# A vision tower with routed experts on one core: token rows read in pieces and turned by VectorE's block transpose, not by products with the identity

## The chip, the core and the metric

One Trainium2 chip (trn2), one of its cores. The metric is the device time of one execution in microseconds, and the figure of the kernel is the median of its runs: 129.36 us before the change, of three runs from 128.86 to 130.53. Five engines take part: TensorE (PE: products), VectorE (DVE), ScalarE (ACT), GpSimd (POOL), and SyncE (SP), whose queue issues most DMAs. Each engine has its own instruction list and waits for the others by semaphores.

## The reference

Sixteen images of 96 x 96 x 3 are cut into 36 patches of 16 x 16 x 3 and projected to 256 features; a class token is put ahead, so there are 16 x 37 = 592 tokens. One attention block (16 heads of 16, causal), and one block of eight experts follow, each over the layer-normalised tokens, each added to its input. The last is what the change touches:

```python
x = layernorm(h).reshape(-1, 256)
red = x @ w_red
logits = red @ (wg / max(norm(wg), 1e-4)).T        # 8 experts
idx = argmax(softmax(logits)); scores = softmax(logits)[idx]
hid = gelu(x @ w1[idx] + b1[idx])                  # 256 -> 1024
y = hid @ w2[idx] + b2[idx]                        # 1024 -> 256
out = h + y * scores
```

Everything is float32. Each token goes to one expert only, so the kernel sorts the tokens by expert and gives each expert the rows it needs.

## The kernel before, in words

It is one program with one hand-written instruction list an engine; no scheduler moves anything. Its stages are the embedding, the first normalisation with value rows, keys and queries, a loop over eight pairs of images (attention), the second normalisation with the choice of the expert, the dispatch, and the expert stage.

**Slots.** A token's row in `hz` holds 640 floats: the residual row h (256), the normalised row z (256), and 128 more, of which the first is the token's number and the second its score (`ROW`, L58). Each expert has a region of `slot_scratch` in DRAM. At the start SyncE clears 112 rows of each region from `nil` (L340). GpSimd scatters the rows of all tokens to their slots (`spread`, L1228). When all five scatters have landed, SyncE reads 112 slots of every expert, 2560 bytes a row, to one buffer an expert (`load_rows`, L363; experts 2, 3, 0, 1, then 4 to 7). `CAP` = 112 slots are a tile; more tokens for an expert would give further tiles, which are behind a condition.

**Experts 0 and 1** do not wait for that: `dispatch` makes their turned rows by products on chip, into `xt`. For **experts 2 to 7** TensorE must turn the normalised half of the rows, slots on partitions, into features on partitions: `turn_rows` (L792 to L801) multiplies by the identity, four products of 64 columns by 112, each "x2" in the trace. VectorE copies the result from PSUM to `xt` (`rows_turned`, L1103 to L1108), which has two buffers.

**The expert stage on TensorE** is `hidden(t)` (L803 to L822: 32 products with w1, moving operand `xt` with 112 columns) and `down(t)` (L824 to L836: 16 products with w2, 256 columns). ScalarE's Gelu stands between. The order is hidden 0, 1, down 0, 1, hidden 2, and then hidden(t), down(t - 1) for t from 3 on. `turn_rows(2)` stands in the middle of `down(1)`, `turn_rows(3)` behind it, and `turn_rows(t + 1)` between `hidden(t)` and `down(t - 1)`. VectorE's `result(t)` (L1110 to L1125) adds bias, score and residual row, which it reads from the gathered rows; GpSimd scatters it to `out` (L1233).

**Weights.** w1 and w2 of an expert are 1 MB each, in a ring of four. Those of experts 0 to 3 are issued during attention; `load_expert(t)` for t from 4 on waits until `down(t - 4)` is done (`y_ps`, L334). All of it is on SyncE's queue, behind the row loads.

**The values** take a path over DRAM: `hz` to `v_scratch` (L344), and back in six loads each half, three of 32 rows by 8 images and three of 5 rows by 8 images (L350; `SPLIT`, L82). **The bias products** (L578 to L582) make a bias of the expert choice from `boutc`; VectorE copies it (L1030).

Of the kernel before, what the change touches and what calls it, by code (L numbers as in the profile page):

```python
# [20 lines left out]
P = 128  # L21
# [23 lines left out]
CAP = 112  # L45
HALVES = ((0, 64), (64, CAP))
# [11 lines left out]
ROW = 2 * D + 128  # L58
# [69 lines left out]
def vit_tower(nc, embed_in, places_in, b_proj, w_qkv, b_qk, b_v, w_out, w_out_t, b_out, b_out_c, wg, w_red_t, w1, b1, w2, b2,  # L128
              cf_d, cb_d, iota_d, out):
    ctx = ExitStack()  # L130
    with ctx:
# [75 lines left out]
        hz = sb("hz", [P, NT, ROW])  # L207
# [5 lines left out]
        hz_id = hz[:, :, :].bitcast(U32)[:, :, 2 * D]  # L213
        hz_score = hz[:, :, 2 * D + 1]
# [36 lines left out]
        xt = late(2 * KD * CAP).rearrange("p (b k n) -> p b k n", b=2, k=KD)  # L251
        yout = pos[:, 0:2, :]
        hsum = sb("hsum", [P, 2, D])

        def row_of(t):
            r = t % E
            return rows[0:CAP, r, :] if r < RING else more[0:CAP, r - RING, :]
# [5 lines left out]
        vrow = hz[:, :, 0:D]  # L263
        v3 = [w[0:GS, RING - 1, :, :].rearrange("p a b -> p (a b)").rearrange("p (b d) -> p b d", d=D)
# [16 lines left out]
        def o_bank(u):  # L281
# [13 lines left out]
            xt_ps xt_ready hidden_ps gelu_ready y_ps y_ready  # L295
# [8 lines left out]
        gathered = [sem(f"gathered{t}") for t in range(E)]  # L304

# [13 lines left out]
        def _(sp):  # L319
# [20 lines left out]
            sp.dma_start(of_expert[0:CAP, :, :], nil[0:CAP, :].unsqueeze(1).to_broadcast([CAP, E, ROW]))\  # L340
# [21 lines left out]
            def load_rows(t):  # L362
                sp.dma_start(row_of(t), of_expert[0:CAP, t, :]).then_inc(gathered[t], 16)  # L363

            sp.wait_ge(q["spread"], 16 * NT)
            for t in (*range(ONCHIP, RING), *range(ONCHIP), *range(RING, E)):
                load_rows(t)
            for t in range(RING, E):
                load_expert(t)
            sp.wait_ge(q["meta_ready"], 1)  # L370
            n = sp.value_load(meta[0:1, 2 * OVF:2 * OVF + 1], min_val=0, max_val=OVF)
            with sp.If(n > 0):
                for t in range(E):
                    sp.wait_ge(gathered[t], 16)
                for i in range(OVF):
                    sp.dma_start(of_expert[(i + 1) * CAP:(i + 2) * CAP, :, :], nil[0:CAP, :].unsqueeze(1).to_broadcast([CAP, E, ROW]))\
                      .then_inc(q["spill_cleared"], 16)
                sp.wait_ge(q["spread"], 16 * 2 * NT)
            for i in range(OVF):
                with sp.If(n > i):  # L380
                    e = sp.value_load(meta[0:1, i:i + 1], min_val=0, max_val=E - 1)
                    row = sp.value_load(meta[0:1, OVF + i:OVF + i + 1], min_val=0, max_val=(E + 1) * APART - CAP)
# [3 lines left out]
                                 w1[bass.ds(e, 1)].rearrange("o (k p) f -> p (o k) f", p=P)).then_inc(loaded_w1[r], 16)  # L386
# [7 lines left out]
                    sp.dma_start(row_of(E + i), slot_d[bass.ds(row, CAP), :]).then_inc(gathered[i], 16)  # L394
# [4 lines left out]
        def _(act):  # L399
# [109 lines left out]
            for t in range(ONCHIP):  # L509
                act.wait_ge(q["soon_ps"], KD * t + 1)  # L510
                nc.scalar.activation(xt[:, t, 0, :], ps[:, BX[t][0], 0:CAP], ACT.Copy).then_inc(q["soon0_ready"], 1)
# [28 lines left out]
        def _(pe):  # L540
# [26 lines left out]
            for j in range(NT):  # L567
# [3 lines left out]
                if j == NT - 2:  # L571
# [71 lines left out]
            turn_normalised(1)  # L643
            value_rows(0)
# [667 lines left out]
```

## Time and profile before

| | us |
|---|---|
| median of the runs | 129.36 |
| range of the three runs | 128.86 to 130.53 |
| the profiled execution, its time | 130.33 |
| its span, from the first to the last instruction | 128.4 |
| TensorE busy in it | 120.5 |
| VectorE, ScalarE, GpSimd busy | 56.7, 48.1, 42.7 |

The time holds 1.9 us that lie around the span. TensorE's granted clock is 0.999 of full speed (2.4 GHz) over the whole span. In the views an engine's name with a q (SPq) is its queue of DMA issues; "ps<-early,w1s" reads as output and inputs; early, wide, w1s, w2s and hz are memory on chip, and `early` holds the row buffers of experts 0 to 3, `gt` and `xt` in this stage, `wide` the row buffers of 4 to 7. A wait's releaser is what ended it. The mean duration of a product overlaps its neighbours, so the length of a stage is read from the chain of waits, not from the sum of means.

### The profile page before, as it was taken

The numbers are of one execution on the slowest core, as the hardware profiler recorded it, in microseconds if no ns is written. First come the engines' busy times: TensorE is split into PE (matmuls) and PEld (weight loads), VectorE is DVE, ScalarE is ACT, GpSimd is POOL, SyncE is SP. The second block draws the span as 40 slices with busy tenths as digits, with TensorE's granted clock in tenths as the row PEclk, the third lists the DMA queues.
The fourth block names the chain that finished last, engine by engine and source line by source line (L and its number), as shares of the span: only waits on it lengthen the run. The fifth ranks groups of instructions, "written<-read, shape, count | busy, mean of one in ns | idle before, by whom it ended". The sixth has DMA issues, their size and how long they took to land.

```text
span 128.4 us, 3559 instructions
## 1 busy us (share of the span) xinstructions
PE 120.5 (94%) x1460; PEld 102.0 (79%) x1460; DVE 56.7 (44%) x178; ACT 48.1 (37%) x145; POOL 42.7 (33%) x58
## 2 busy tenths in 40 slices
PE   7969999999999999999999899999999999999970
PEld 2747887877667878798799798899898999999850
DVE  1140599661996858798987300160212121220210
ACT  0300002447486666666456760036333150606000
POOL 8800014590059039272857800032020202011022
PEclk9999999999999999999999999999999999999999
DMA  4899999137919999999999947999999999200011
GB/s 114 289 334 385 390 405 394 67 125 174 171 36 205 149 269 360 390 365 379 365 402 369 362 141 212 321 298 343 381 378 384 362 388 333 68 5 25 3 29 31
DMA packets 19681, 32.75 MB, mean 255 GB/s; under 512 B 1779, under 2 KB 13686, under 8 KB 19662
## 3 DMA queue, kind: packets, MB, share of 16 engines
q1 hardware_dynamic: 18126, 30.06, 72.2%
q0 software_dynamic: 768, 2.12, 4.6%
q10 hardware_dynamic: 768, 0.31, 0.9%
q8 instruction: 13, 0.21, 0.7%
q14 instruction: 6, 0.05, 0.1%
HBM read 27.41 MB, written 5.38 MB: 255 GB/s over the span
## 4 chain that ended last, share of the span: by engine, by line
PE 68%; DMA 15%; issue 8%; POOL 3%; SPq 2%; ACT 1%; DVE 1%; POOLq 0%
PE ps L818 18%; PE ps L834 16%; PE ps L543 9%; DMA w2s<-v_scratch 6%; DMA early<-embed_in 5%; DMA v_scratch<-hz 4%; PE ps L734 4%; PE ps L602 4%; PE ps L690 3%; PE ps L703 3%; PE ps L609 3%; PE ps L799 2%; POOL vbd L1186 2%; PE ps L672 2%; POOL out L1233 1%
## 5 line engine op out<-in xcount | busy, mean ns | idle before, releaser
L834 PE MATMUL ps<-w2s,early 128*64 128x256 f32 (+1 forms) x256 | 29.2, 379 | 0.0
L525 ACT ACTIVATE early<-ps,b1s 128x112 f32<-128x112 f32 x64 | 17.4, 354 | 30.4 <-PE ps L818 30.4
L818 PE MATMUL ps<-early,w1s 128*64 128x112 f32 x512 | 26.1, 259 | 0.5 <-issue 0.5
L818 PEld LDWEIGHTS ps<-early,w1s 128*64 128x64 f32 x512 | 25.6, 137 | 1.0 <-issue 0.8
L834 PEld LDWEIGHTS ps<-w2s,early 128*64 128x64 f32 (+1 forms) x256 | 23.1, 130 | 3.4
L543 PE MATMUL ps<-early 128*128 128x256 f32 x60 | 15.0, 403 | 1.3 <-DMA early<-embed_in 1.2
L543 PEld LDWEIGHTS ps<-early 128*128 128x128 f32 x60 | 11.6, 200 | 4.1 <-DMA early<-embed_in 2.6
L1106 DVE COPY early<-ps 128x224 f32<-128x224 f32 x6 | 2.4, 392 | 24.4 <-PE ps L799 24.4
L1233 POOL DMA_INDIRECT out<-pos,early x4 | 3.8, 943 | 24.7 <-DVE pos L1124 24.4
L1233 POOL DMA_INDIRECT out<-pos,wide x4 | 3.8, 942 | 20.0 <-DVE pos L1124 20.0
L609 PE MATMUL ps<-xnt,wqkv 128*128 128x296 f32 x32 | 9.1, 422 | 0.0
L935 DVE TENSOR_REDUCE negmax<-ps 101x16 f32<-101x592 f32 x8 | 6.2, 774 | 5.8 <-PE ps L635 5.7
L410 ACT ACTIVATE xnt<-ps 128x256 f32<-128x256 f32 x5 | 1.7, 381 | 17.7 <-PE ps L589 17.7
L1158 POOL TENSOR_TENSOR rstd<-veps,cf 128x1 f32<-128x1 f32 x5 | 3.2, 632 | 15.4 <-DVE veps L883 15.4
L1124 DVE SCALAR_TENSOR_TENSOR pos<-ps,wide,hsum 112x256 f32<-112x256 f32 x4 | 1.9, 484 | 13.7 <-issue 13.7
L690 PEld LDWEIGHTS ps<-vbd,probst 111*64 111x64 f32 (+1 forms) x192 | 6.1, 125 | 1.4 <-issue 0.9
L609 PEld LDWEIGHTS ps<-xnt,wqkv 128*128 128x128 f32 x32 | 5.8, 190 | 1.8 <-issue 0.2
L690 PE MATMUL ps<-vbd,probst 111*64 111x51 f32 (+2 forms) x192 | 6.7, 215 | 0.4
L447 ACT ACTIVATE probs<-probs 101x592 f32<-101x592 f32 x8 | 5.6, 697 | 3.0 <-DVE probs L939 2.9
L1186 POOL TENSOR_TENSOR vbd<-w1s,cf 111x512 f32<-111x512 f32 x4 | 4.1, 1056 | 7.8 <-DMA w1s<-v_scratch 7.8
L672 PE MATMUL ps<-cf,probs 101*111 101x101 f32 x48 | 6.2, 266 | 0.2 <-ACT probs L447 0.2
L479 ACT ACTIVATE probst<-ps 111x303 f32<-111x303 f32 x16 | 5.9, 428 | 1.3 <-PE ps L672 1.3
(141 smaller groups left out, 172.7 us busy)
## 6 DMA issues: line engine op xcount, KB each, us to landing
w1s<-w SPq DMA_DIRECT2D x8, 1024.0 KB, 9.9
w2s<-w SPq DMA_DIRECT2D x8, 1024.0 KB, 12.7
early<-embed_in SPq DMA_DIRECT2D x5, 448.0 KB, 7.8
slot_scratch<-nil SPq DMA_DIRECT2D x1, 2240.0 KB, 14.6
early<-slot_scratch SPq DMA_DIRECT2D x4, 280.0 KB, 4.1
wide<-slot_scratch SPq DMA_DIRECT2D x4, 280.0 KB, 6.3
b2s<-b SPq DMA_DIRECT2D x4, 256.0 KB, 7.8
wqkv<-w_qkv SPq DMA_DIRECT2D x1, 768.0 KB, 11.0
```

The lines of the kernel that those rows point to most:

```text
L447: nc.scalar.activation(probs[:, u % 2, 0:ALLS], probs[:, u % 2, 0:ALLS], ACT.Exp).then_inc(q["probs_ready"], 1)
L479: nc.scalar.activation(probst[:, u % 2, half * GH * ROWS:(half + 1) * GH * ROWS], ps[0:GS, BP + half, 0:GH * ROWS], ACT.Copy).then_inc(q[" ...
L525: nc.scalar.activation(gt[:, t % 2, f, :], ps[:, 2 * (t % 2) + f // 4, (f % 4) * CAP:(f % 4 + 1) * CAP], ACT.Gelu, bias=b1t[:, f:f + 1]).t ...
L543: return nc.tensor.matmul(ps[:, j, 0:D], emb[:, k, D + j * P:D + (j + 1) * P], emb[:, k, 0:D], start=(k == 0), stop=(k == KE - 1))
L609: m = nc.tensor.matmul(ps[:, QK_BANK[a][n], 0:HALF], wqkv[:, k, col:col + P], xnt[:, k, a * HALF:(a + 1) * HALF], start=(k == 0), stop=(k ...
L672: m = nc.tensor.transpose(ps[0:GS, BP + half, g * ROWS:(g + 1) * ROWS], probs[:, u % 2, at:at + GS], ident[0:ROWS, 0:ROWS])
L690: m = nc.tensor.matmul(ps[a * ROW_B:a * ROW_B + w, o_bank(u), g * GH * VW:g * GH * VW + n], probst[:, u % 2, at:at + w], vbd[:, col:col + ...
L818: m = nc.tensor.matmul(ps[a * ROW_B:(a + 1) * ROW_B, 2 * (t % 2) + f // 4, (f % 4) * CAP:(f % 4 + 1) * CAP], w1s[:, r, k, c:c + ROW_B], xt ...
L834: m = nc.tensor.matmul(ps[n0:n1, 4 + t % 2, 0:D], gt[:, t % 2, f, n0:n1], w2s[:, r, f, :], start=(f == 0), stop=(f == FT - 1))
L935: link(V.tensor_reduce(negmax[:, u % 2, :].rearrange("p (r h) -> p r h", r=2), s3, AX.X, ALU.max, negate=True))
L1186: pool.tensor_tensor(vbd[:, 2 * u * VI:2 * (u + 1) * VI].rearrange("p (h w) -> p h w", w=VW)[:, :, 0:DH], v3[g][:, b0:b0 + 2, :].rearrange ...
L1233: pool.indirect_dma_start(out, bass.IndirectOffsetOnAxis(row_of(t).bitcast(U32)[:, 2 * D:2 * D + 1], 0), yout[0:CAP, t % 2, :], None, boun ...
```

## The change

- **Rows by pieces.** In a token's row the 128 extra floats now stand ahead, with the number at 127 and the score at 126 (`AHEAD`), so that score, number and residual row are 258 floats in a row. For experts from 2 on the normalised half comes by a load of its own, `load_blocks`: 128 slots, each cut into 4 runs of 64 floats (256 bytes), so that partition 32 b + a holds the run b of slots 4 a to 4 a + 3. `load_rows` brings the other 258 floats (1032 bytes) of 112 slots, for experts from 2 on in the order i, a of slot 4 a + i. Experts 0 and 1 read them in the plain order.
- **The turning** is one STREAM_TRANSPOSE of VectorE an expert, 128 x 256, blocks of 32 x 32, from the buffer straight to `xt`; `turn_rows` and its semaphore are gone. `xt` has 128 columns instead of 112, in four runs of 32 of which 28 are read. A feature's place is now 2 p + k, so w1 of these experts is loaded as "(p k) f", 8 KB in a row for each partition.
- **The order of the queue.** Blocks of 2 and 3 and rows of 0 to 3 come first; those of 4 and 5 behind the weights of 4, those of 6 and 7 behind the weights of 5.
- **Clearing** takes 128 slots of each expert instead of 112.
- **The bias products** move from the embedding to behind `turn_normalised(1)`. These are the four small products of the trace (two instructions, "x4").

```diff
+QB = 32
+NQ = P // QB
+CA = CAP // NQ
...
-ROW = 2 * D + 128
+AHEAD = 128
+ROW = AHEAD + 2 * D
...
-        xt = late(2 * KD * CAP).rearrange("p (b k n) -> p b k n", b=2, k=KD)
+        xt = late(2 * KD * P).rearrange("p (b k n) -> p b k n", b=2, k=KD)
...
+        def slots_of(t, k):
+            if t < ONCHIP:
+                return xt[:, t, k, 0:CAP]
+            return xt[:, t % 2, k, :].rearrange("p (i a) -> p i a", i=NQ)[:, :, 0:CA]
...
-                sp.dma_start(w1s[:, r, :, :], w1[t].rearrange("(k p) f -> p k f", p=P)).then_inc(loaded_w1[r], 16)
+                of_chunks = "(k p) f -> p k f" if t < ONCHIP else "(p k) f -> p k f"
+                sp.dma_start(w1s[:, r, :, :], w1[t].rearrange(of_chunks, p=P)).then_inc(loaded_w1[r], 16)
...
-            sp.dma_start(of_expert[0:CAP, :, :], nil[0:CAP, :].unsqueeze(1).to_broadcast([CAP, E, ROW]))\
+            sp.dma_start(of_expert[0:P, :, :], nil[:, :].unsqueeze(1).to_broadcast([P, E, ROW]))\
...
-            def load_rows(t):
-                sp.dma_start(row_of(t), of_expert[0:CAP, t, :]).then_inc(gathered[t], 16)
+            def load_blocks(t, slots):
+                sp.dma_start(blocks_of(t).rearrange("p (i n) -> p i n", i=NQ),
+                             slots[:, AHEAD + D:ROW].rearrange("s (b n) -> b s n", b=NQ)).then_inc(blocks_in[t % E], 16)
+
+            def load_rows(t, slots):
+                cols = slice(AHEAD - 2, AHEAD + D)
+                if t < ONCHIP:
+                    sp.dma_start(row_of(t)[:, cols], slots[0:CAP, cols]).then_inc(gathered[t], 16)
+                else:
+                    sp.dma_start(row_of(t)[:, cols], slots[0:CAP, cols].rearrange("(a i) n -> i a n", i=NQ))\
+                      .then_inc(gathered[t % E], 16)
 
             sp.wait_ge(q["spread"], 16 * NT)
-            for t in (*range(ONCHIP, RING), *range(ONCHIP), *range(RING, E)):
-                load_rows(t)
+            for t in range(ONCHIP, RING):
+                load_blocks(t, of_expert[0:P, t, :])
+            for t in range(RING):
+                load_rows(t, of_expert[0:P, t, :])
             for t in range(RING, E):
                 load_expert(t)
+                if t < RING + 2:
+                    for a in (2 * t - RING, 2 * t - RING + 1):
+                        load_blocks(a, of_expert[0:P, a, :])
+                        load_rows(a, of_expert[0:P, a, :])
...
-                    pe.wait_ge(q["loaded_boutc"], 16)
-                    for k in range(KD):
-                        m = nc.tensor.matmul(bo_ps, boutc[:, k:k + 1].to_broadcast([P, P]), Gc[:, k, :],
-                                             start=(k == 0), stop=(k == KD - 1))
-                    m.then_inc(q["wg_ps"], 1)
...
             turn_normalised(0)
             turn_normalised(1)
+            pe.wait_ge(q["loaded_boutc"], 16)
+            for k in range(KD):
+                m = nc.tensor.matmul(bo_ps, boutc[:, k:k + 1].to_broadcast([P, P]), Gc[:, k, :],
+                                     start=(k == 0), stop=(k == KD - 1))
+            m.then_inc(q["wg_ps"], 1)
             value_rows(0)
...
-            def turn_rows(t):
-                pe.wait_ge(gathered[t % E], 16 * (t // E + 1))
-                if t >= ONCHIP + 2:
-                    pe.wait_ge(q["xt_ready"], t - ONCHIP - 1)
-                for k in range(KD):
-                    for a in range(2):
-                        c = D + k * P + a * ROW_B
-                        m = nc.tensor.matmul(ps[a * ROW_B:(a + 1) * ROW_B, 6 + t % 2, k * CAP:(k + 1) * CAP],
-                                             row_of(t)[:, c:c + ROW_B], ident[0:CAP, 0:CAP], start=True, stop=True)
-                m.then_inc(q["xt_ps"], 1)
...
-                                w1s[:, r, k, c:c + ROW_B], xt[:, t % 2, k, :], start=(k == 0), stop=(k == KD - 1))
+                                w1s[:, r, k, c:c + ROW_B], slots_of(t, k), start=(k == 0), stop=(k == KD - 1))
...
-                    if t == 1 and f == FT // 2:
-                        turn_rows(2)
...
-            turn_rows(3)
             hidden(2)
             for t in range(3, E):
                 hidden(t)
-                if t + 1 < E:
-                    turn_rows(t + 1)
...
             def rows_turned(t):
-                dve.wait_ge(q["xt_ps"], t - ONCHIP + 1)
+                dve.wait_ge(blocks_in[t % E], 16 if t < E + ONCHIP else 32)
                 dve.wait_ge(q["hidden_ps"], 2 * (t - 1))
-                V.tensor_copy(xt[:, t % 2, :, :],
-                              ps[:, 6 + t % 2, 0:KD * CAP].rearrange("p (k n) -> p k n", k=KD))\
-                    .then_inc(q["xt_ready"], 1)
+                V.transpose(xt[:, t % 2, :, :].rearrange("p k (i a) -> p k i a", i=NQ),
+                            blocks_of(t).rearrange("p (i c k) -> p k i c", i=NQ, c=QB)).then_inc(q["xt_ready"], 1)
```

SyncE's queue from the wait for the scatter on, before (x4 and x8 are counts; `slot_scratch` is the slots in DRAM):

```order
L335 DMA w1s<-w 128x2x1024
L336 DMA w2s<-w 128x8x256
L363 DMA early<-slot_scratch 112x640 x4
L363 DMA wide<-slot_scratch 112x640 x4
L335 DMA w1s<-w 128x2x1024
L336 DMA w2s<-w 128x8x256
L335 DMA w1s<-w 128x2x1024
L336 DMA w2s<-w 128x8x256
```

and with the change (shapes are those of the side that is written):

```order
L381 DMA early<-slot_scratch 128x4x64 x2
L387 DMA early<-slot_scratch 112x258 x2
L389 DMA early<-slot_scratch 112x1x258 x2
L353 DMA w1s<-w 128x2048
L354 DMA w2s<-w 128x8x256
L381 DMA wide<-slot_scratch 128x4x64
L389 DMA wide<-slot_scratch 112x1x258
L381 DMA wide<-slot_scratch 128x4x64
L389 DMA wide<-slot_scratch 112x1x258
L353 DMA w1s<-w 128x2048
L354 DMA w2s<-w 128x8x256
```

Eight whole loads stood ahead of the weights of expert 4; now six smaller ones do, and four stand between the weights of 4 and those of 5. The same four follow behind the weights of 5.

TensorE from the embedding's last products to the first value rows, before:

```order
L543 MATMUL ps<-early 128x256 x12
L576 MATMUL ps<-wqkv,woutt 128x8 x4
L580 MATMUL ps<-wqkv,boutc 128x8 x2
L543 MATMUL ps<-early 128x256 x3
L589 MATMUL ps<-cf,hz 128x128 x4
L602 MATMUL ps<-wqkv,xnt 128x264 x2
```

and with the change:

```order
L579 MATMUL ps<-early 128x256 x12
L612 MATMUL ps<-wqkv,woutt 128x8 x4
L579 MATMUL ps<-early 128x256 x3
L620 MATMUL ps<-cf,token_rows 128x128 x4
L677 MATMUL ps<-wqkv,boutc 128x8 x2
L633 MATMUL ps<-wqkv,xnt 128x264 x2
```

The two products with `boutc` moved behind the turning of two tiles and stand ahead of the first value rows.

## Rows read from the trace of the kernel before

**Rows 1.** The page: busy time, 40 slices, issues (KB each, us to landing).

```profile
span 128.4 us, 3559 instructions
...
PE 120.5 (94%) x1460; PEld 102.0 (79%) x1460; DVE 56.7 (44%) x178; ACT 48.1 (37%) x145; POOL 42.7 (33%) x58
...
PE   7969999999999999999999899999999999999970
...
DMA  4899999137919999999999947999999999200011
...
w1s<-w SPq DMA_DIRECT2D x8, 1024.0 KB, 9.9
...
early<-slot_scratch SPq DMA_DIRECT2D x4, 280.0 KB, 4.1
```

**Rows 2.** The chain of waits, expert stage: start us, us, what.

```profile
...
81.18 0.39 PE ps L799 x8
...
83.68 6.14 PE ps L818 x128
89.82 0.39 PE ps L799 x8
90.20 3.46 PE ps L834 x32
93.66 3.07 PE ps L818 x64
...
107.47 3.07 PE ps L818 x64
```

**Rows 3.** VectorE's timeline: start us, us, engine, line, operation, tiles, count, idle before.

```profile
...
97.15 0.39 DVE L1106 COPY early<-ps 128x224 f32<-128x224 f32 x1 [2.91 <-PE ps L799]
...
100.66 0.48 DVE L1124 SCALAR_TENSOR_TENSOR pos<-ps,early,hsum 112x256 f32<-112x256 f32 x1 [2.73 <-issue]
```

**Rows 4.** SyncE's queue, timeline of its DMA issues: start us, us.

```profile
...
25.78 0.37 SPq L344 DMA_DIRECT2D v_scratch<-hz  x1
...
76.88 1.76 SPq L363 DMA_DIRECT2D early<-slot_scratch  x4
...
80.56 0.64 SPq L335 DMA_DIRECT2D w1s<-w  x1
...
83.33 2.32 SPq L335 DMA_DIRECT2D w1s<-w  x1
...
93.69 0.37 SPq L335 DMA_DIRECT2D w1s<-w  x1
```

**Rows 5.** DMA view of 76.8 to 79 us, busy tenths in 40 slices.

```profile
...
DMA  0000000000000000000995773907256979699999
```

**Rows 6.** DMA view of 94 to 98 us.

```profile
...
DMA packets 1105, 1.47 MB, mean 367 GB/s; under 512 B 27, under 2 KB 987, under 8 KB 1105
```

**Rows 7.** DMA view of 34 to 37.3 us, busy tenths of 16 engines in 40 slices.

```profile
...
DMA  9998876533433233333311200000000000000000
```

**Rows 8.** DMA view of 9.5 to 12 us: packets, MB, share of 16 engines.

```profile
...
q1 hardware_dynamic: 269, 0.92, 92.7%
q10 hardware_dynamic: 241, 0.00, 5.3%
```

**Rows 9.** DMA view of 32 to 34 us.

```profile
...
q1 hardware_dynamic: 379, 0.36, 115.9%
```

**Rows 10.** The chain of waits before the attention loop.

```profile
...
19.64 0.45 PE ps L580 x4
...
21.48 0.23 PE ps L589 x2
...
21.73 0.39 ACT xnt L410
...
22.17 1.16 PE ps L602 x4
```

**Rows 11.** DMA view of 22 to 25 us.

```profile
...
DMA  8998988765663432112111100000000700000000
```

More of the change, by code:

```diff
@@ L206, in vit_tower @@
         shift2 = sb("shift2", [P, NT])
-        hz = sb("hz", [P, NT, ROW])
+        token_rows = sb("token_rows", [P, NT, ROW])
+        hz = token_rows[:, :, AHEAD:ROW]
         nil = sb("nil", [P, ROW])
@@ L212, in vit_tower @@
         one = nc.const_aps.tensor(1.0, (P, 1), BF16)
-        hz_id = hz[:, :, :].bitcast(U32)[:, :, 2 * D]
-        hz_score = hz[:, :, 2 * D + 1]
+        hz_id = token_rows[:, :, :].bitcast(U32)[:, :, AHEAD - 1]
+        hz_score = token_rows[:, :, AHEAD - 2]
         lg = sb("lg", [P, NT, E])
@@ L250, in vit_tower, with buffer_of, blocks_of @@
         gt = late(2 * FT * CAP).rearrange("p (b f n) -> p b f n", b=2, f=FT)
-        xt = late(2 * KD * CAP).rearrange("p (b k n) -> p b k n", b=2, k=KD)
+        xt = late(2 * KD * P).rearrange("p (b k n) -> p b k n", b=2, k=KD)
         yout = pos[:, 0:2, :]
         hsum = sb("hsum", [P, 2, D])
+        def buffer_of(t):
+            r = t % E
+            return rows[:, r, :] if r < RING else more[:, r - RING, :]
         def row_of(t):
-            r = t % E
-            return rows[0:CAP, r, :] if r < RING else more[0:CAP, r - RING, :]
+            return buffer_of(t)[0:CAP, :]
+        def blocks_of(t):
+            return buffer_of(t)[:, AHEAD + D:ROW]
         w1s = sb("w1s", [P, RING, KD, F])
@@ L294, in vit_tower @@
             nil_ready slots_cleared ids_ready spread spill_cleared soon_ps soon0_ready soon1_ready count_ps count_ready hsum_ready
-            xt_ps xt_ready hidden_ps gelu_ready y_ps y_ready
+            xt_ready hidden_ps gelu_ready y_ps y_ready
             meta_ready
@@ L304, in vit_tower @@
         gathered = [sem(f"gathered{t}") for t in range(E)]
+        blocks_in = [sem(f"blocks_in{t}") for t in range(E)]
         block = ctx.enter_context(nc.Block())
@@ L374, in _ @@
                     sp.wait_ge(gathered[t], 16)
+                for t in range(ONCHIP, E):
+                    sp.wait_ge(blocks_in[t], 16)
                 for i in range(OVF):
-                    sp.dma_start(of_expert[(i + 1) * CAP:(i + 2) * CAP, :, :], nil[0:CAP, :].unsqueeze(1).to_broadcast([CAP, E, ROW]))\
+                    sp.dma_start(of_expert[(i + 1) * P:(i + 2) * P, :, :], nil[:, :].unsqueeze(1).to_broadcast([P, E, ROW]))\
                       .then_inc(q["spill_cleared"], 16)
@@ L381, in _ @@
                     e = sp.value_load(meta[0:1, i:i + 1], min_val=0, max_val=E - 1)
-                    row = sp.value_load(meta[0:1, OVF + i:OVF + i + 1], min_val=0, max_val=(E + 1) * APART - CAP)
+                    row = sp.value_load(meta[0:1, OVF + i:OVF + i + 1], min_val=0, max_val=(E + 1) * APART - P)
                     r = (E + i) % RING
@@ L393, in _ @@
                     sp.wait_ge(scattered[i % 2], 16 * (i // 2 + 1))
-                    sp.dma_start(row_of(E + i), slot_d[bass.ds(row, CAP), :]).then_inc(gathered[i], 16)
+                    load_blocks(E + i, slot_d[bass.ds(row, P), :])
+                    load_rows(E + i, slot_d[bass.ds(row, P), :])
             for b in range(2):
@@ L510, in _ @@
                 act.wait_ge(q["soon_ps"], KD * t + 1)
[L511 removed]
+                nc.scalar.activation(xt[:, t, 0, 0:CAP], ps[:, BX[t][0], 0:CAP], ACT.Copy).then_inc(q["soon0_ready"], 1)
             act.wait_ge(q["low_ready"], 1)
@@ L854, in _ @@
                     with pe.If(n > i):
-                        turn_rows(E + i)
                         hidden(E + i)
@@ L869, in _ @@
             V = nc.vector
-            V.memset(nil[:, 0:2 * D], 0.0)
+            V.memset(nil[:, AHEAD:ROW], 0.0)
             dve.wait_ge(q["loaded_cf"], 16)
@@ L886, in norm_apply @@
                 return V.tensor_scalar(dst, src, m[:, j, 0:1], rs[:, j:j + 1], ALU.subtract, ALU.mult)
-            V.memset(nil[:, 2 * D + 1:ROW], 0.0).then_inc(q["nil_ready"], 1)
-            V.tensor_copy(nil[:, :].bitcast(U32)[:, 2 * D:2 * D + 1], C("norow")).then_inc(q["nil_ready"], 1)
+            V.memset(nil[:, 0:AHEAD - 1], 0.0).then_inc(q["nil_ready"], 1)
+            V.tensor_copy(nil[:, :].bitcast(U32)[:, AHEAD - 1:AHEAD], C("norow")).then_inc(q["nil_ready"], 1)
             V.tensor_copy(hz_id, C("tok")).then_inc(q["ids_ready"], 1)
@@ L1076, in _ @@
                 dve.wait_ge(q["soon_ps"], KD * (t + 1))
-                V.tensor_copy(xt[:, t, 1, :], ps[:, BX[t][1], 0:CAP]).then_inc(q["soon1_ready"], 1)
+                V.tensor_copy(xt[:, t, 1, 0:CAP], ps[:, BX[t][1], 0:CAP]).then_inc(q["soon1_ready"], 1)
             scores_of(BY_PE, NT)
@@ L1148, in _ @@
             pool.memset(qt[:, :, T:TP], 0.0)
-            pool.memset(hz[:, :, 2 * D + 2:ROW], 0.0)
+            pool.memset(token_rows[:, :, 0:AHEAD - 2], 0.0)
             pool.memset(ot[:, :, T:TP], 0.0)
@@ L1232, in scatter @@
                 pool.wait_ge(q["y_ready"], t + 1)
-                pool.indirect_dma_start(out, bass.IndirectOffsetOnAxis(row_of(t).bitcast(U32)[:, 2 * D:2 * D + 1], 0), yout[0:CAP, t % 2, :], None,
+                pool.indirect_dma_start(out, bass.IndirectOffsetOnAxis(row_of(t).bitcast(U32)[:, AHEAD - 1:AHEAD], 0), yout[0:CAP, t % 2, :], None,
                                         bounds_check=last_token, oob_is_err=False).then_inc(scattered[t % 2], 16)
```

10 lines of the change are left out of this document (5 added, 5 removed).

## The prediction

> **What bounds the kernel now.** I read the page first [rows 1]: TensorE is busy for 120.5 of 128.4 us and in nearly every slice, and the DMA digits stand at 9 from the 24th slice to the 34th. So TensorE is the bound, and the transfers run at their limit beside it for some 35 us; a change here must be judged on both. Next the chain of waits in the expert stage [rows 2]: it is TensorE alone. A first product of an expert (`hidden`, L818) takes 3.07 us, a second one (`down`, L834) 3.46 us, a turning of rows (`turn_rows`, L799) 0.39 us, one after the other without a gap. VectorE waits in the same stretch [rows 3]: two gaps of 2.91 and 2.73 us an expert. Then the queue that loads [rows 4]: the row loads are issued at 76.88 us, when the scatter of token rows has landed, the weights of expert 4 at 80.56, those of 5 at 83.33, of 6 at 93.69. A load of w1 lands 9.9 us after its issue [rows 1], so 6's is there at about 103.5 us, while `hidden(6)` starts at 107.47 [rows 2]: 4 us of slack. That slack is what the change draws on.
>
> **What goes.** Six `turn_rows` leave TensorE: 6 x 0.39 = 2.34 us of a gapless chain, all of it on the path. The two bias products (L580, "x4" in the trace) are moved. Before, they took 0.45 us inside the embedding [rows 10]; now they stand behind the turning of tiles 0 and 1, where TensorE waited for ScalarE's copy from 21.71 to 22.17 us (21.48 + 0.23 to 22.17). TensorE comes there 0.45 us earlier, but the products stand ahead of the value rows, and VectorE's normalised tiles are no earlier. The start of the value rows moves from 22.17 to about 21.92, a gain of 0.25 us. I carry it through the attention loop, where the path runs over the first value rows; if it is lost there, the sum is 0.25 us worse.
>
> **What costs nothing, and its cover.** The block transpose takes the place of the COPY of 0.39 us [rows 3]. Taken at 0.4 us; even at four times that, 1.6 us, it fits VectorE's gap of 2.91 us, since it stands where `hidden` of the expert before has 3 us to go and `down` 3.46. Were the gap gone, it would delay the next `hidden` by its length. The clearing of the slots writes 128 rows, not 112: 1/7 more of 2240 KB, 0.33 MB or 0.9 us at 367 GB/s [rows 6]. Before, it is over by about 23.9 us [rows 11], and the queue's next transfer is issued at 25.78 [rows 4]: 0.9 fits in 1.9 us. w1 in longer pieces carries the same bytes: nothing. The moving operand of `hidden` now has runs of 28 columns with gaps. No row shows such an operand; I take 3.07 us as before, and put the doubt with the rivals.
>
> **What is added: transfers by pieces.** An expert from 2 on gets its normalised half by `load_blocks`, 512 pieces of 256 bytes, and the rest by `load_rows`, 112 pieces of 1032 bytes. The bytes are fewer than the 280 KB of before. What counts is how many DMA engines carry them. The trace shows that it can be few [rows 7]: after the 32-row loads of the value scratch are done, the busy share stands at 3 tenths for a dozen slices, and only then dies out. 5 of 16 engines are 0.31, and the loads still under way are those of 5 rows (L350, the second of each pair). All three sit on the same five engines, or the share would be higher. The new transfers have 4 as the outermost length on the side they read (the four column blocks, and the four residues of the row number) and 128 or 112 on the side they write. I take it that they run on 4 engines, the same four each time. The trace has no transfer whose two sides differ, so this is a reading, not a row. The Trainium skill ("DMA: Bandwidth & Descriptors", Why a DMA increments its semaphore by 16 and not by 1) says that the number of engines is the largest up to 16 that divides the slowest dimension of both sides, and that on such a queue they are the lowest-numbered. By that rule it is 4; the trace agrees as far as it goes [rows 7].
>
> **Price of a piece.** From 9.5 to 12 us one queue moved 269 packets of 0.92 MB in 92.7% of 16 engines' time, the other 241 tiny ones in 5.3% [rows 8]. That is 37.1 us / 269 = 138 ns for 3420 bytes, and 2.1 us / 241 = 8.8 ns for nearly none: 8.8 ns and 0.0378 ns a byte. So 18.5 ns for 256 bytes and 47.8 for 1032. The upper end is the value loads [rows 9]: 115.9% of 32 us / 379 = 98 ns for 950 bytes, where the line says 45: double. I take 20 and 50 ns, near the low end, since the value loads write to few partitions at a time and these to all. The Trainium skill (the same page, its table of key numbers) gives 512 bytes as the least for full rate; priced as 512 bytes a block piece would take 28 ns, and the sum below would be 6.1 us longer. No run here shows that yet.
>
> **The sum, on one of the four engines.** They hold 1/16 of the weights and 1/4 of every piecewise load, in the order of the queue:
> - the start: 76.88 less 0.25, and the first packet about 1 us behind the issue [rows 5]: 77.6 us;
> - blocks of experts 2 to 7: 6 x 128 x 0.020 = 15.4 us;
> - rows of 2 to 7: 6 x 28 x 0.050 = 8.4 us; rows of 0 and 1 go by 16 engines, 14 x 0.050 = 0.7;
> - weights of 4 and 5: 2 x 2.10 MB at 367 GB/s [rows 6] = 11.4 us; w1 of 6: 2.9;
> - three scatters of results that pass through meanwhile, 7 rows of 1 KB each: 1.0.
>
> Sum 39.8 us, so w1 of expert 6 is there at 117.4 us. The queue stands in this order because the change issues blocks and rows of 4 and 5 behind the weights of 4, and those of 6 and 7 behind the weights of 5; none of its issues comes too late to keep these engines fed. Without the wait `hidden(6)` would start at 107.47 - 0.25 - 5 x 0.39 = 105.3 us. Ahead of it lie smaller waits that this one swallows: the blocks of 4 are there at 77.6 + 5.1 + 0.7 + 2.8 + 5.7 + 2.6 = 94.5 us, plus 0.4 of transpose, and `hidden(4)` wants them at 92.2. Blocks 2 and 3 come at 80.2 and 82.7, in time. From `hidden(6)` on TensorE has 2 x 3.07 + 3 x 3.46 = 16.5 us of work: 117.4 + 16.5 = 133.9 us, against 107.47 + 0.39 + 16.5 = 124.4 before. **+9.5 us.** w1 of 7 comes 5.7 us behind, while `hidden(6)` and `down(5)` take 6.5: no further wait. The profiled execution's own time is 130.33 us, so it would be 139.8; on the median of 129.36 us it is **138.9 us**.
>
> **The rivals.**
> - *The pieces go over 16 engines* (or 8), because the side that is written decides: 0.15. A block load is then 32 pieces of 20 ns on an engine, 0.64 us, all pieces together 6.7 us, and the bytes are fewer than before. No wait arises, and only 2.34 + 0.25 = 2.6 us go: 126.8 us, faster, just at 2%. For it speaks that all transfers with 128 or 112 rows on both sides fill the engines; against it the tail of the value loads [rows 7]. It decides at 8 engines: then the pieces take 11.9 + 0.7 us instead of 24.5, and w1 of 6 lands at 105.5 us, the time at which it is wanted.
> - *Pieces at double price on four engines*: + 768 x 18 ns + 168 x 48 ns = 22 us, 161 us: 0.03. Halfway to it, 150.
> - *The rows of 1032 bytes over 16, the blocks alone over 4*: 6.3 us less, 132.6 us; 0.03, slower all the same.
> - *The gaps in the moving operand halve its rate*: 6 x 3.07 = 18.4 us more than the 126.8: 145 us; 0.01.
>
> **How the numbers follow.** 0.78 for the forecast; its own range is 135 (18.5 and 47.8 ns and no scatter: 2.6 us less, and 1 us for the median's scatter) to 150. With the rival of 132.6 the range is 132 to 151, which leaves out the fast rival and the doubled price, 0.18 in all. 2% of 129.36 us is 2.6 us, about what a measurement of this kernel tells from no change. Slower by over 2%: 0.78 + 0.03 + 0.03 + 0.01 = 0.85, less 0.02 for slack that I do not see, 0.83. The fast rival lands on the border of 2%: 0.08 faster, 0.09 the same.
>
> **What the profile after would show.** Right: the DMA share at 2 to 4 tenths over long stretches between 82 and 120 us, where it was 9; landings of the blocks some 3 us apart for experts 2 and 3; TensorE idle ahead of `hidden(4)` by 2 to 3 us and ahead of `hidden(6)` by about 6, released by a DMA or by the transpose; VectorE waiting for `early` or `wide` from `slot_scratch`; the end of the chain still scatter and landing. Wrong: a share of 9 that ends before 107 us, L799's 2.34 us gone and nothing in its place. The price is wrong if the 128 pieces of a block load take other than 2.6 us from the first landing to the next; the reading of the moved products is wrong if the first value row starts at 22.17 us as before.

## The result, and the profile after

The change makes the kernel slower: 141.8 us (median of 4 runs, 141.01 to 143.17) against 129.38 us (4 runs of before on the same chip), ratio 1.0901 [1.0842, 1.096]. 138.9 us had been predicted, in a range of 132 to 151. The profiled execution took 141.01 us with a span of 139.2; that of before 130.33 and 128.4. So the two profiles differ by 10.7 to 10.8 us, which is what the traces can explain; the medians lie 12.4 us apart, because before's profiled execution is one of its longer ones and this one is the shortest of its kernel. Here and below a ratio is taken over the undisturbed (fast) runs alone, so it need not be the quotient of the two medians, which is 1.096 here.

Page of the changed kernel: span, busy time, 40 slices of 3.5 us each, one group of instructions.

```profile
span 139.2 us, 3465 instructions
...
PE   7898989999999999999999999933999904999980
...
PEclk9999999999999999999999999998699975799997
DMA  4989997369299999999994149942894499960000
...
L1125 DVE STREAM_TRANSPOSE early<-wide 128x256 f32<-128x256 f32 x4 | 1.8, 446 | 17.0 <-DMA wide<-slot_scratch 17.0
```

Against [rows 1], TensorE has two holes (slices 27 and 28, then 33 and 34), its clock sags at each, and the DMA digits stand at 4 and 2 in slices 27 and 28 and at 4 and 4 in slices 31 and 32, in a stretch where they stood at 9. (The low digits of slices 22 and 23, around the wait for the scatter, have their like in [rows 1].) A transpose takes 0.45 us, on an engine with time to spare.

The chain of waits of the changed kernel: start us, us, what.

```profile
21.86 0.99 PE ps L633 x4
...
72.47 3.88 DMA slot_scratch<-token_rows,keyu
76.36 0.69 SPq L381
...
84.89 8.63 SPq L389
...
96.95 0.47 SPq L353
...
98.57 7.69 SPq L389
...
109.90 6.78 DMA w1s<-w
116.72 4.93 PE ps L843 x64
```

Where [rows 2] show TensorE alone, the path now runs over SyncE's queue and the load of w1 of expert 6, and only from 116.72 us over TensorE again. The value rows (L633) start at 21.86 us; it was 22.17 [rows 10].

TensorE's timeline of the same stretch: start us, us, engine, line, operation, tiles, count, idle before and what ended it. L843 is `hidden`, L857 `down`.

```profile
96.38 4.86 PE L843 MATMUL ps<-early,w1s 128*64 128x112 f32 x64 [4.69 <-issue]
101.05 3.64 PE L857 MATMUL ps<-w2s,early 128*64 128x256 f32 x32
104.51 3.25 PE L843 MATMUL ps<-early,w1s 128*64 128x112 f32 x64
107.57 3.64 PE L857 MATMUL ps<-w2s,early 128*64 128x256 f32 x32
116.72 4.93 PE L843 MATMUL ps<-early,w1s 128*64 128x112 f32 x64 [5.51 <-DMA w1s<-w]
...
128.00 7.07 PE L857 MATMUL ps<-w2s,early 128*64 128x256 f32 x64
```

The two waits stand ahead of `hidden(4)` and `hidden(6)`, as forecast, and nowhere else. The product behind each takes 4.9 us, the undisturbed ones (expert 5) 3.25. TensorE ends at 135.07 us (128.00 + 7.07). Before, it ended at 124.4, by the last line of its timeline:

```profile
117.22 7.13 PE L834 MATMUL ps<-w2s,early 128*64 128x256 f32 x64
```

The 10.7 us of the profiles are all here.

VectorE's timeline, the transposes (answering [rows 3]).

```profile
80.68 0.45 DVE L1125 STREAM_TRANSPOSE early<-early 128x256 f32<-128x256 f32 x1 [9.21 <-DMA early<-slot_scratch]
82.69 0.45 DVE L1125 STREAM_TRANSPOSE early<-early 128x256 f32<-128x256 f32 x1 [1.57 <-DMA early<-slot_scratch]
...
95.83 0.45 DVE L1125 STREAM_TRANSPOSE early<-wide 128x256 f32<-128x256 f32 x1 [10.89 <-DMA wide<-slot_scratch]
```

Blocks 2 and 3 are there at 80.7 and 82.7 us (80.2 and 82.7 forecast), blocks 4 at 95.8 (94.5 forecast). `hidden(4)` starts at 96.38 us, 0.1 us behind the end of its transpose.

DMA view of 78 to 80 us: busy tenths of 16 engines, rate, the queue's packets, MB and share.

```profile
DMA  0132212112100023333333232333333333323333
GB/s 0 26 72 67 56 36 51 41 46 51 26 0 5 15 61 77 72 72 72 72 72 77 67 77 67 77 72 77 72 72 72 72 72 72 77 67 77 72 72 77
...
q1 hardware_dynamic: 463, 0.12, 25.9%
```

These are the block loads of experts 2 and 3; no other piece passes in this window. Both are issued by 78.5 us, and yet the share stays at 2 to 3 tenths and the rate at 72 GB/s, against 367 in [rows 6].

The same view of 108 to 109.1 us, rows of expert 6.

```profile
DMA  3314431111133223133231323346111122451121
...
q1 hardware_dynamic: 71, 0.07, 23.3%
```

Windows of the changed kernel: us, PE busy (instructions), PEld, DVE, ACT, POOL, granted clock, DMA share, GB/s.

```profile
82.60:83.40 0.80, 0.80 (x22) 0.80 (x19) 0.70 (x2) 0.00 (x0) 0.00 (x0) 1.00 0.17 37
94.40:95.00 0.60, 0.00 (x0) 0.00 (x0) 0.00 (x0) 0.00 (x0) 0.00 (x0) 1.00 0.12 29
...
96.30:98.50 2.20, 2.12 (x24) 2.15 (x26) 0.82 (x2) 0.00 (x0) 0.94 (x1) 0.50 0.42 83
...
111.25:116.70 5.45, 0.00 (x0) 0.00 (x0) 1.29 (x3) 0.00 (x0) 0.94 (x1) 0.69 0.97 311
116.70:118.50 1.80, 1.78 (x20) 1.78 (x22) 0.00 (x0) 0.00 (x0) 0.00 (x0) 0.50 1.10 394
118.50:121.50 3.00, 3.00 (x50) 3.00 (x50) 0.00 (x0) 1.09 (x4) 0.00 (x0) 0.73 1.02 387
121.50:125.00 3.50, 3.50 (x38) 2.24 (x36) 0.00 (x0) 1.09 (x4) 0.00 (x0) 1.00 0.68 221
```

In the wait of 5.5 us the clock falls to its lower level, 1.2 GHz (0.50), and it is back at 2.4 GHz only some 3 us after work has begun again. The wait costs its own length and then 1.7 to 1.9 us more. The first two windows show two stretches, 1.4 us in all, in which the DMA engines move about half the 72 GB/s or less; they are taken up again with the sum.

### The profile page after: what moved, and what is told of

It reads as the page before. It is cut to its first block, busy times and chain, and to the rows that moved or that the text cites. A ratio compares the mean times of both kernels' runs of the same rounds, so it can differ in the third digit from the quotient of the medians.

```text
span 139.2 us, 3465 instructions
## 1 busy us (share of the span) xinstructions
PE 121.4 (87%) x1412; PEld 98.5 (71%) x1412; DVE 56.7 (41%) x178; ACT 48.2 (35%) x145; POOL 42.7 (31%) x58
## 4 chain that ended last, share of the span: by engine, by line
SPq 29%; DMA 25%; PE 22%; issue 10%; DVE 6%; POOL 5%; POOLq 0%; ACT 0%; DVEq 0%
SPq L389 17%; DMA woutt<-w_out_t 8%; DMA w2s<-v_scratch 6%; DMA w1s<-w 5%; PE ps L843 4%; DMA v_scratch<-token_rows 4%; PE ps L633 3%; SPq L381 3%; PE ps L640 3%; DMA slot_scratch<-token_rows,keyu 3%; POOL slot_scratch L1246 3%; PE ps L857 2%; PE ps L726 2%; SPq L387 2%; SPq L340 2%
## 5 line engine op out<-in xcount | busy, mean ns | idle before, releaser
L843 PE MATMUL ps<-early,w1s 128*64 128x112 f32 x512 | 29.2, 278 | 10.4 <-DMA w1s<-w 5.5
L843 PEld LDWEIGHTS ps<-early,w1s 128*64 128x64 f32 x512 | 28.3, 150 | 11.9 <-DMA w1s<-w 6.0
L857 PE MATMUL ps<-w2s,early 128*64 128x256 f32 (+1 forms) x256 | 28.8, 379 | 0.0
L857 PEld LDWEIGHTS ps<-w2s,early 128*64 128x64 f32 (+1 forms) x256 | 19.7, 130 | 6.9
L579 PE MATMUL ps<-early 128*128 128x256 f32 x60 | 14.5, 391 | 1.1 <-DMA early<-embed_in 1.0
L1125 DVE STREAM_TRANSPOSE early<-wide 128x256 f32<-128x256 f32 x4 | 1.8, 446 | 17.0 <-DMA wide<-slot_scratch 17.0
## 6 DMA issues: line engine op xcount, KB each, us to landing
w2s<-w SPq DMA_DIRECT2D x8, 1024.0 KB, 12.4
```

The source lines that it names most:

```text
L579: return nc.tensor.matmul(ps[:, j, 0:D], emb[:, k, D + j * P:D + (j + 1) * P], emb[:, k, 0:D], start=(k == 0), stop=(k == KE - 1))
L843: m = nc.tensor.matmul(ps[a * ROW_B:(a + 1) * ROW_B, 2 * (t % 2) + f // 4, (f % 4) * CAP:(f % 4 + 1) * CAP], w1s[:, r, k, c:c + ROW_B], sl ...
L857: m = nc.tensor.matmul(ps[n0:n1, 4 + t % 2, 0:D], gt[:, t % 2, f, n0:n1], w2s[:, r, f, :], start=(f == 0), stop=(f == FT - 1))
```

## The experiments

Three theories were to be told apart from the start. **Few engines**: a load whose outermost length is 4 on one side runs over 4 of the 16 engines, and the weights' share on those four queues behind it. **Small pieces**: the 256-byte pieces are dear wherever they go. **Transpose**: the loss is the wait for VectorE's block transpose as such. Each ratio is against the kernel before on the same chip in the same set; the chips differ (before took 132.95 to 133.66 us in the first eight, 129.22 in the last three), so microseconds are compared inside a set.

**Blocks over 16 engines** (e1_blocks_16). The same 256-byte pieces, asked for with 32 as the outermost length on both sides; rows as in the change.

```diff
-sp.dma_start(blocks_of(t).rearrange("p (i n) -> p i n", i=NQ),
-             slots[:, AHEAD + D:ROW].rearrange("s (b n) -> b s n", b=NQ))
+for b in range(NQ):
+    c = AHEAD + D + b * (D // NQ)
+    sp.dma_start(blocks_of(t)[b * QB:(b + 1) * QB, :].rearrange("p (i n) -> p i n", i=NQ),
+                 slots[:, c:c + D // NQ].rearrange("(a i) n -> a i n", i=NQ))
```

> The changed kernel with each block load cut into four DMAs, one a column block: 32 partitions outermost on the side that is read and on the side that is written, the same 512 pieces of 256 bytes. The row loads of experts 2 to 7 stay as they are (outermost length 4 on the side that is read). Theory 'few engines': the block loads now go over 16 engines, 0.6 us an expert instead of 2.4; the rows alone leave w1 of expert 6 at about 105 us, where it is wanted, so nearly the whole loss is gone: 126 to 129 us, ratio to before 0.98 to 1.00. Theory 'small pieces' (256-byte pieces are what is slow, on however many engines): as many pieces, so 138 to 142 us, ratio 1.07 to 1.10. Theory 'transpose' (the wait for VectorE's block transpose as such): unchanged, 1.09.

135.24 us against 132.95, ratio 1.0144 [1.0009, 1.0278]: most of the loss is gone with the pieces unchanged in size and number, and small pieces at 1.07 or more are out. But it is not at 0.98 either. TensorE's timeline and SyncE's queue (start us, us, issues) show why:

```profile
112.89 3.29 PE L845 MATMUL ps<-early,w1s 128*64 128x112 f32 x64 [2.32 <-DMA w1s<-w]
```

```profile
85.00 5.07 SPq L383 DMA_DIRECT2D wide<-slot_scratch  x4
...
90.87 4.06 SPq L383 DMA_DIRECT2D wide<-slot_scratch  x4
...
106.58 0.47 SPq L353 DMA_DIRECT2D w1s<-w  x1
```

Four issues for an expert's blocks hold the queue 4 to 5 us, w1 of 6 is issued only at 106.58 and landed at 112.9, where [rows 4] have it issued at 93.69. Here the queue that issues is a part of the cause, with the rows on four engines.

**Rows over 16 engines, moving operand restrided** (e2_rows_16).

```diff
-return xt[:, t % 2, k, :].rearrange("p (i a) -> p i a", i=NQ)[:, :, 0:CA]
+return xt[:, t % 2, k, :].rearrange("p (i a) -> p a i", i=NQ)[:, 0:CA, :]
...
-sp.dma_start(row_of(t)[:, cols], slots[0:CAP, cols].rearrange("(a i) n -> i a n", i=NQ))
+sp.dma_start(row_of(t)[:, cols], slots[0:CAP, cols])
```

> The changed kernel with the row loads of experts 2 to 7 in plain order (112 rows outermost on both sides, so 16 engines); to match it the moving operand of the first products is read in slot order, with a stride of 32 floats. The block loads stay on four engines. Theory 'few engines': 6.3 us less on the four engines, so w1 of expert 6 is there at about 111 us instead of 116.7: 134 to 136 us, ratio 1.03 to 1.055. Theory 'small pieces': the 256-byte pieces are untouched and are the cause: 140 to 142 us, ratio 1.08 to 1.10. If the strided moving operand costs TensorE its rate, it is far slower than the change, over 1.15.

148.65 us, ratio 1.1167 [1.1007, 1.1328]: the strided operand does cost TensorE its rate, though less than the "over 1.15", and the run is of no use on the rows. TensorE's timeline has no wait ahead of any `hidden` from expert 2 on, and a `hidden` of twice the length:

```profile
99.76 6.46 PE L839 MATMUL ps<-early,w1s 128*64 128x112 f32 x64
106.00 3.68 PE L853 MATMUL ps<-w2s,early 128*64 128x256 f32 x32
```

6.24 us from start to start at a full clock, against 3.06 in the change (104.51 to 107.57, above). What differs for TensorE is the order in which the moving operand is read: neighbours 32 floats apart here, runs of 28 neighbours there. The Trainium skill ("SBUF — State Buffer", Door 1: The DMA port swizzle) says that SBUF is read in lines of 16 bytes and needs at least two hits in a line for the full rate; by that rule a step of 32 floats is slow and runs of 28 are not, and these two runs agree.

**Blocks and rows over 16, in plain order** (e3_both_16). The block load takes the slots so that the transpose leaves them in order; the moving operand is then without gaps.

```diff
-return xt[:, t % 2, k, :].rearrange("p (i a) -> p i a", i=NQ)[:, :, 0:CA]
+return xt[:, t % 2, k, 0:CAP]
...
+                 slots[:, c:c + D // NQ].rearrange("(i a) n -> a i n", i=NQ))
...
+sp.dma_start(row_of(t)[:, cols], slots[0:CAP, cols])
```

> Both kinds of piece loads over 16 engines: block loads as four DMAs of 32 partitions, a partition 32 b + a now holding slots 32 i + a, so that the transpose leaves the slots in plain order; row loads plain; the moving operand without gaps. Pieces, transpose, order of the queue and the moved products as in the change. Theory 'few engines': no DMA wait is left and the 2.34 us of the turning products plus about 0.4 us of the moved products are won: 126 to 127.5 us, ratio 0.975 to 0.985; granted clock 1.0. 'Small pieces' or 'transpose': 138 us or more, ratio over 1.06.

131.74 us, ratio 0.9876 [0.9763, 0.9989]. No wait is left ahead of the `hidden` of experts 2 to 7; around expert 6 (`down(4)`, then `hidden(6)`) TensorE's timeline reads

```profile
105.88 3.65 PE L855 MATMUL ps<-w2s,early 128*64 128x256 f32 x32
109.33 3.27 PE L841 MATMUL ps<-early,w1s 128*64 128x112 f32 x64
```

The transposes, the six products fewer and the 256-byte pieces are all still there, so small pieces and transpose are out. This kernel differs from the change in more than the number of engines (four DMAs for one, no gaps in the operand), so the opposite test is needed too.

**The kernel before, with its whole rows on four engines** (e4_before_rows_on_4). The opposite test: no small piece, 2560 bytes each.

```diff
-sp.dma_start(row_of(t), of_expert[0:CAP, t, :]).then_inc(gathered[t], 16)
+sp.dma_start(row_of(t), of_expert[0:CAP, t, :].rearrange("(a i) n -> i a n", i=4)).then_inc(gathered[t], 16)
```

(for experts 2 to 7)

> The kernel before with one edit: the whole-row loads of experts 2 to 7 (2560 bytes a piece, no small piece) are read in the order i, a of slot 4 a + i, outermost length 4 on the side that is read, 112 on the side that is written. TensorE's turning, VectorE and all else as before. Theory 'few engines': 28 pieces of 105 ns an expert on each of four engines, 6 x 2.9 us + 1.5 us ahead of the weights of expert 4, whose w1 is then there at about 100 us instead of 93.7, and TensorE's clock falls in the wait: 135 to 138 us, ratio 1.045 to 1.07. 'Small pieces' and 'transpose': no change, ratio 1.00.

144.52 us, ratio 1.0828 [1.0684, 1.0973]. The order of an access pattern alone, with the bytes and rows of before, costs 8%, a little more than the 1.045 to 1.07 expected. With e3_both_16 this shows it: the distribution over engines made the change slow. Chain of waits:

```profile
85.00 19.43 DMA w1s<-w
104.47 5.99 PE ps L821 x64
```

w1 of expert 4 needs 19.4 us from issue to landing behind those rows (100 us was expected for its landing, 104.4 it was), and the `hidden` behind the wait of 8.4 us takes 5.99 us, at a granted clock of 0.50 from 104.5 to 108 us: the term that the forecast lacked, here too.

**The good version again, in five rounds** (e5_both_16_again; the kernel of e3_both_16).

> The kernel of e3 once more, in five rounds, beside the others of this set. 'Few engines': with the piece loads on 16 engines the 2.34 us of the turning products and 0.47 us of the moved products are won, 2.8 us in all: ratio 0.975 to 0.985. e3 gave 0.988 with a wide interval, and its profile has small gaps in the first two experts. If the ratio is again near 0.99, about 1 us of the 2.8 is given back somewhere.

130.64 us against 133.66, ratio 0.977 [0.9702, 0.9839]: 3.0 us faster than before, and faster than the change. `turn_rows` (2.34) and the moved products (0.47, as expected before the run) make 2.8.

**The moved products alone** (e6_moved_only; the kernel before with the two bias products behind `turn_normalised(1)`).

> The kernel before with the two bias products alone moved behind the turning of tile 1. In the profile of the change the first products of expert 0 start at 68.43 us instead of 68.90. If that comes from the move: 0.4 to 0.5 us faster, ratio 0.996 to 0.997. If it was chance of one execution: 1.000. My prediction had 0.25 us, ratio 0.998.

132.71 us against 133.66, ratio 0.9937 [0.9889, 0.9985]: a small gain, 0.2 to 1.5 us, which holds the 0.4 to 0.5 expected.

**The clock held up** (e7_filled). The change, with products that nobody reads ahead of `hidden(4)` and `hidden(6)`.

```diff
+def fill(n):
+    for _ in range(n):
+        nc.tensor.matmul(ps[:, BZ, :], one.to_broadcast([P, P]), one.to_broadcast([P, 2 * D]), start=True, stop=True)
...
+fill({4: 18, 6: 24}.get(t, 0))
 hidden(t)
```

> The change with products that nothing reads (128 x 512, bf16, to a PSUM bank that is free there) put into TensorE's two long waits: 18 ahead of the first products of expert 4, 24 ahead of those of expert 6, each about 0.21 us, so some 3.8 and 5.1 us, less than the waits of 8.4 (4.7 of it without any record) and 5.5 us. Theory 'clock': TensorE's granted clock fell to 0.5 after the waits, and the first products of expert 6 took 4.93 us instead of 3.1; kept busy, it keeps 1.0, and 1.5 to 1.9 us at the end are won: ratio 1.075 to 1.08 instead of 1.09, granted clock 0.99 or more. The same loss behind the first wait is swallowed by the second. Rival: the products of expert 6 were slow for another reason (transfers that write beside them): no gain, 1.09.

141.06 us, ratio 1.0535 [1.045, 1.062]. `hidden(6)` is back at full rate:

```profile
112.35 5.42 PE L863 MATMUL ps<-const-bfloat16-1.0 128*128 128x512 bf16 x24
117.70 3.29 PE L843 MATMUL ps<-early,w1s 128*64 128x112 f32 x64
```

The ratio is lower than the 1.075 to 1.08 expected, but it can't be held against the 1.09 of the result: on this chip the kernel before is 4 us longer, and the change itself was not run there. So it was run again beside the change (below).

**Rows over 16, unpaired** (e8_rows_16_unpaired). The rows' load in plain order with the moving operand of the change; the results are joined to another slot's score and residual row, so the output is another.

> The change with the row loads of experts 2 to 7 in plain order and so over 16 engines, while the expert's products keep the other order of the slots, with the moving operand of the change: each result is joined to the score and the residual row of another slot. Block loads on four engines as in the change. It replaces e2, where the strided operand hid the answer. 'Few engines': 6.3 us less work on the four engines ahead of w1 of expert 6, which is there at about 110.5 us instead of 116.7: 134.5 to 136.5 us on the first chip, ratio 1.03 to 1.05. 'Small pieces': 1.09.

135.63 us (131.7 to 136.61) against 133.66; no ratio can be given with so much scatter. TensorE's timeline:

```profile
95.58 3.29 PE L839 MATMUL ps<-early,w1s 128*64 128x112 f32 x64 [1.82 <-issue]
...
111.52 4.95 PE L839 MATMUL ps<-early,w1s 128*64 128x112 f32 x64 [2.67 <-DMA w1s<-w]
```

w1 of 6 lands at 111.5 us (110.5 expected), 5.2 us before the change's 116.7 (on another chip). Its first block load is issued at 75.32 us instead of 76.36, so some 4.2 us are left for the rows on the four engines, for the 6.3 of the rival. The times scatter too much to test the 1.03 to 1.05. The last line shows one thing more: a wait of only 2.67 us was followed by a `hidden` of 4.95 us, while in e1_blocks_16 one of 2.32 us was followed by 3.29 us, at a full clock.

**The change again, and filled again** (e9_change_again, e10_filled_again), side by side on a chip on which before takes 129.22 us.

> The change itself, so that e7 and e10 have it beside them on one chip. On the chips of e1 to e8 the kernel before takes 133 to 133.7 us, and the profiles of e1 to e7 show TensorE halting in the first products of experts 0 and 1 and its clock at 0.5 from 74 to 77 us; the change waits for DMA later and should swallow that. If so, the change takes 141 to 143 us on such a chip too, and its ratio falls from 1.09 to 1.06 to 1.07; on a chip like the first it is 1.09. If the halt comes on top: 145 us or more.

> The kernel of e7, now beside the change. 'Clock': 1.5 to 1.9 us less than e9, a ratio 0.012 to 0.015 lower, and the first products of expert 6 in 3.3 us instead of 4.9. Rival: the same time as e9.

The change: 141.65 us, ratio 1.0962 [1.0883, 1.1041], as in the result. What it does on a chip with the longer time of before stayed untested, since this one is not such a chip. Filled: 140.81 us, 1.0857 [1.0756, 1.0958]. The gain is 0.84 us in the medians and 0.0105 in the ratio, where 1.5 to 1.9 us and 0.012 to 0.015 were expected, and the intervals overlap. The timelines, first of the change, then filled, are clearer:

```profile
117.04 4.59 PE L843 MATMUL ps<-early,w1s 128*64 128x112 f32 x64 [6.07 <-DMA w1s<-w]
...
127.99 7.07 PE L857 MATMUL ps<-w2s,early 128*64 128x256 f32 x64
```

```profile
116.88 3.29 PE L843 MATMUL ps<-early,w1s 128*64 128x112 f32 x64 [0.30 <-DMA w1s<-w]
...
126.51 7.08 PE L857 MATMUL ps<-w2s,early 128*64 128x256 f32 x64
```

w1 lands at the same time in both, and the last products end 1.5 us earlier in the second. That the half clock delays TensorE's end by 1.5 us is shown; that all of it reaches the kernel's time is not (the two spans, 139.2 and 139.3 us, are alike). The traces show where these two executions lose it again: the last scatter of results starts at 135.93 us in the change and at 134.45 in the filled kernel, but from issue to landing it takes (DMA views of 134 to 140 us, first the change)

```profile
out<-pos,wide POOLq DMA_INDIRECT x1, 2.5
```

```profile
out<-pos,wide POOLq DMA_INDIRECT x1, 4.1
```

Why the landing is later is open.

**Weights of 5 and 6 ahead of the pieces** (e11_weights_first). Blocks and rows of 4 and 5 are issued behind the weights of 5, those of 6 and 7 behind the weights of 6.

```diff
-if t < RING + 2:
-    for a in (2 * t - RING, 2 * t - RING + 1):
+if t in (RING + 1, RING + 2):
+    for a in (2 * t - RING - 2, 2 * t - RING - 1):
```

> The change with the order of the queue shifted: blocks and rows of experts 4 and 5 behind the weights of 5 instead of those of 4, those of 6 and 7 behind the weights of 6. Same loads, same four engines. The sum over the four engines says: blocks of 4 are there at about 100 us, so hidden(4) waits 5 us longer than in the change, but w1 of expert 6 comes at about 109 us and the blocks of 6 at 113 to 115; then TensorE runs on, with w1 of 7 at about 121. The end comes 2 to 4 us earlier than in the change: 138 to 140 us where the change takes 141.8. Rival: each wait adds up, so the longer first wait makes it 4 to 6 us slower than the change.

141.08 us (138.02 to 141.61) against 129.22; no ratio is given. The one wait has moved to where the sum on four engines puts it:

```profile
101.08 6.22 PE L843 MATMUL ps<-early,w1s 128*64 128x112 f32 x64 [9.94 <-issue]
...
126.68 7.09 PE L857 MATMUL ps<-w2s,early 128*64 128x256 f32 x64
```

From there on nothing waits, and TensorE ends at 133.77 us, 1.3 before the change where 2 to 4 were expected; the rival, 4 to 6 us slower, is out. In this execution the last scatter again lands late, 4.4 us after its issue. The order on the queue decides where the wait stands, hardly how long the work on the four engines is; and the longer wait cost a longer stretch at half clock (6.22 us for `hidden(4)`).

## Why the prediction was right, and where its sizes were off

**The mechanism held.** Four engines: the plateau of 72 GB/s at a share of 0.26, e3_both_16, which takes the loss away with the same pieces, and above all e4_before_rows_on_4, which brings it about by the outermost length alone. The rule of the Trainium skill for the number of engines that was cited in the forecast ("DMA: Bandwidth & Descriptors", Why a DMA increments its semaphore by 16 and not by 1) agrees with these runs. The rival of 16 engines falls, and so does the one of gaps in the moving operand: with runs of 28, `hidden` takes its 3.06 us.

**The sum came out at 133.9 us for TensorE's end; it was 135.07.** That it came so close is in part luck, since errors in both directions cancel. Term by term:
- *w1 of 6 at 117.4*: 116.72, 0.7 earlier. Behind the near hit two prices are off in opposite directions. At 72 GB/s over four engines a block piece of 256 bytes takes 256 / 18 = 14.2 ns of an engine's time (17.9 by the packets' own durations, 25.9% of 32 us / 463, so they overlap a little): 768 of them are 10.9 us, not 15.4. A row piece of 1032 bytes took 4 x 1.1 us / 71 = 62 ns from 108 to 109.1 us, not 50: 168 of them are 10.4 us, not 8.4. By the forecast's own sign the block price was wrong: from the landing of blocks 2 to that of blocks 3 it is 2.0 us (80.68 to 82.69), not 2.6. The sum of both is 2.5 us under the forecast, the landing only 0.7. For most of the other 1.8 an estimate from the views finds two places. The start took about 0.7: the plateau begins only at 78.65 us, behind 0.65 us at half that rate, where the forecast had 77.6. The stretches of 37 and 29 GB/s at 82.6 and 94.4 us took about 0.7 together. What left the engines short of work in them is not shown.
- *The 512 bytes* for full rate that the Trainium skill ("DMA: Bandwidth & Descriptors", table of key numbers) gives would have made a block piece 28 ns by the forecast's estimate: not borne out by any stretch here, and e3_both_16 hides 3072 such pieces altogether.
- *16.5 us behind `hidden(6)`'s start*: 18.35 (116.72 to 135.07). **This is the step that was missing**: the wait of 5.51 us is followed by a stretch at half clock, 4.93 instead of 3.07 us for the product behind it, 1.86 us. Nothing in the forecast asked what TensorE does after a hole. e10_filled_again shows it by taking it away.
- *The start 0.25 us earlier*: value rows 0.31 earlier (21.86 for 22.17). In e6_moved_only the whole kernel gains 0.2 to 1.5 us; the sign is right, the size was on the low side.
- *The transpose at 0.4 us under cover*: 0.45, covered.
- *`hidden(4)` waits 2 to 3 us*: 4.69, since blocks 4 came 1.3 later than 94.5 and `down(2)` ended half a microsecond before the 92.2 expected. As said, the later wait swallowed it, but it left its own 1.6 us at half clock (4.67 us from `hidden(4)` to the next product, for 3.06).
- *"None of its issues comes too late"*: too bold. One issue of row pieces held SyncE's queue for 8.63 us and another for 7.69, so that the weights of 5 were issued at 96.95 and those of 6 at 109.90. In the change most of it is covered, as the four engines are still at the pieces (blocks of 7 up to about 111 us); in e1_blocks_16 late issues are a part of the cause.
- *A misreading* without effect on the sum: in [rows 1] the DMA digits stand at 4 and 7 in slices 24 and 25 and at 9 from slice 26 to 34, some 29 us and not 35.

0.7 us less, 1.86 more: 133.9 becomes 135.1. What the medians have beyond that (12.4 for 10.7 us) is in executions without a profile, and stays open.

## What to carry to other kernels

Before giving a DMA a rearranged access pattern, look at the outermost length on both sides: it decides over how many engines the load runs, and a load on few engines delays every later transfer on the queue, since each of those has its share on them. Work it out on one of those engines, not on the total of bytes. And price a wait on TensorE at its length plus what follows at half clock: 1.4 to 1.9 us behind waits of 4.7 to 6.1 us here, 3 us behind the one of 9.94, and 1.9 behind one of only 2.67.

## What the runs showed of the hardware that was not expected

- One DMA issue can hold SyncE's queue for 8.63 us (`L389`) when it stands behind pieces on four engines; the same kind of issue takes 0.7 us in e1_blocks_16, where only the rows are on four engines. The held issue need not be one for few engines: in e8_rows_16_unpaired a row load in plain order was held for 9.91 us behind block loads on four engines.
- A moving operand of f32 with a step of 32 floats halves TensorE's rate (6.24 for 3.06 us); runs of 28 floats with gaps of 4 cost nothing.
- A block transpose of 128x256 f32 on VectorE takes 446 ns, hardly more than the copy that it replaced (390).
- On the chips of the first eight experiments TensorE has small halts between 70.3 and 74.6 us, in five of the eight (e1, e3, e5, e6, e7) followed by a dip of the clock. The page of e5_both_16_again, TensorE and its clock in slices of 3.2 us:

```profile
PE   7989999999999999999999499999999999999970
...
PEclk9999999999999999999999959999999999999998
```

The kernels on the chip of the last three experiments do not show the dip there. As far as these runs tell, it goes with the chip and not with an edit, and it is why only ratios inside one set are compared. Its cause is open.
